# Residual input copied to the output by DMA and accumulated onto, with x reloaded as bf16 and the expert broadcast in another PSUM tile

## The reference

```python
x = x + hgrn(layernorm(x), Wi, Wf, Wg, g_norm_weight, Wo)
x = x + moe(layernorm(x), router_w, w1, w2, w3)

def hgrn(x):                      # all weights 2048 x 2048
    gate = sigmoid(x @ Wf.T); i_in = silu(x @ Wi.T) * (1 - gate)
    o = scan over tokens of o[t] = gate[t] * o[t-1] + i_in[t]
    g = x @ Wg.T
    return (g * rsqrt(mean(g*g) + EPS) * g_norm_weight * (o * sigmoid(o))) @ Wo.T

def moe(x):                       # 8 experts, top 2, d_ff 1024
    weights = softmax of the two largest router logits, 0 for the others
    return sum_e weights[e] * ((silu(x @ w1[e]) * (x @ w2[e])) @ w3[e])
```

## Time and profile before

| | us |
|---|---|
| median of 3 runs | 4249.4 |
| lowest of the runs | 4248.9 |
| the profiled execution | 4253.0 |
| its span on the slowest core (core 5) | 4251.1 |
| spans of the 8 cores | 4232.7 to 4251.1 |
| PE busy | 3777.4 (89%) |
| DVE busy | 1351.3 (32%) |
| ACT busy | 366.5 (9%) |
| POOL busy | 316.2 (7%) |
| mean granted TensorE clock | 0.95 |

### The profile page before, as it was taken

One profiled execution on the slowest core, in us unless ns is written; L12 is line 12 of the kernel. 1 busy time (PEld: TensorE's weight loads), 2 busy tenths in 40 slices (PEclk: granted clock), 3 DMA queues, 4 the chain that ended last, 5 costly groups with the idle time before them and its releaser, 6 DMA issues.

```text
span 4251.1 us, 43621 instructions; the slowest of 8 cores (4232.7 to 4251.1 us)
## 1 busy us (share of the span) xinstructions
PE 3777.4 (89%) x18832; PEld 1776.6 (42%) x18832; DVE 1351.3 (32%) x1154; ACT 366.5 (9%) x347; POOL 316.2 (7%) x358
## 2 busy tenths in 40 slices
PE   0998999989913899999999999999999999999992
PEld 0554444434412344444444444444444444444442
DVE  4322455532245223222222322322322222232233
ACT  3222121110020000000000000000000000000000
POOL 0000000000000001100100100100000010010011
PEclk9998999999956999999999999999999999999995
DMA  5122212112173233433433443344344344334239
GB/s 168 31 35 46 39 30 40 20 35 36 38 228 70 27 38 35 43 35 33 43 36 32 43 40 33 35 43 40 30 40 40 30 40 40 33 38 40 23 35 158
DMA packets 416189, 204.23 MB, mean 48 GB/s; under 512 B 399600, under 2 KB 399600, under 8 KB 407808
## 3 DMA queue, kind: packets, MB, share of 16 engines
q0 software_dynamic: 411216, 167.84, 32.4%
q1 hardware_dynamic: 4784, 33.61, 2.6%
HBM read 302.11 MB, written 33.55 MB: 79 GB/s over the span
## 4 chain that ended last, share of the span: by engine, by line
PE 81%; DVE 9%; DMA 6%; ACT 2%; issue 1%; DVEq 0%; POOL 0%; ACTq 0%; SPq 0%; POOLq 0%
PE pga L862 21%; PE pw L923 21%; PE pva L877 20%; PE po L566 5%; PE pg L327 5%; DMA y<-fsc 3%; PE pi L468 3%; PE pf L468 3%; DMA fsc<-x 2%; DVE fsc L500 2%; DVE fsc L507 1%; DVE bufB L508 1%; DVE bufA L252 1%; ACT fsc L504 1%; DVE fsc L608 0%
## 5 line engine op out<-in xcount | busy, mean ns | idle before, releaser
L862 PE MATMUL pga<-bufA,wsc 128*128 128x512 bf16 x4032 | 908.1, 384 | 12.4 <-DVE fsc L819 12.4
L923 PE MATMUL pw<-gvw,wsc 128*128 128x512 bf16 x4096 | 899.1, 383 | 20.5 <-DVE gvw L896 18.7
L877 PE MATMUL pva<-bufA,wsc 128*128 128x512 bf16 x4032 | 890.8, 379 | 0.0
L923 PEld LDWEIGHTS pw<-gvw,wsc 128*128 128x128 bf16 x4096 | 403.3, 99 | 516.3 <-issue 43.3
L862 PEld LDWEIGHTS pga<-bufA,wsc 128*128 128x128 bf16 x4032 | 398.0, 99 | 503.2 <-issue 39.4
L877 PEld LDWEIGHTS pva<-bufA,wsc 128*128 128x128 bf16 x4032 | 394.5, 98 | 475.7
L742 POOL DMA_DIRECT2D wsc<-w x256 | 258.1, 1009 | 2528.6 <-PE pga L862 1118.5
L935 DVE TENSOR_TENSOR bufB<-pw,bufB 128x1024 bf16<-128x1024 f32 x224 | 274.3, 1225 | 524.4 <-PE pw L923 524.4
L889 DVE TENSOR_TENSOR gvw<-fsc,pga 128x1024 bf16<-128x1024 f32 x126 | 153.9, 1221 | 796.1 <-ACT fsc L885 796.1
L885 ACT ACTIVATE fsc<-pga 128x1024 f32<-128x1024 f32 x126 | 129.1, 1024 | 2474.2 <-PE pga L862 2474.2
L893 DVE TENSOR_TENSOR scr<-pva,fsc 128x1024 bf16<-128x1024 f32 x126 | 154.3, 1225 | 568.2 <-PE pva L877 568.2
(11 more groups left out here) (123 smaller groups left out, 1407.3 us busy)
## 6 DMA issues: line engine op xcount, KB each, us to landing
wsc<-w POOLq DMA_DIRECT2D x128, 512.0 KB, 6.3
fsc<-x SPq DMA_DIRECT2D x32, 1024.0 KB, 6.5
y<-fsc POOLq DMA_DIRECT2D x32, 1024.0 KB, 8.6
wsc<-w POOLq DMA_DIRECT2D x128, 256.0 KB, 4.4
wsc<-wg POOLq DMA_DIRECT2D x16, 512.0 KB, 5.0
wsc<-wo POOLq DMA_DIRECT2D x16, 512.0 KB, 5.0
gvw<-wi POOLq DMA_DIRECT2D x16, 512.0 KB, 5.1
gvw<-wf POOLq DMA_DIRECT2D x16, 512.0 KB, 6.7
```

The lines of the kernel that those rows point to most:

```text
L862: ins = e.matmul(out=pga[:, n2 * 512:(n2 + 1) * 512], lhsT=lhsT, rhs=bufA[:, k * 2048 + nn:k * 2048 + nn + 512], start=(k == 0), stop=(k = ...
L877: ins = e.matmul(out=pva[:, n2 * 512:(n2 + 1) * 512], lhsT=lhsT, rhs=bufA[:, k * 2048 + nn:k * 2048 + nn + 512], start=(k == 0), stop=(k = ...
L923: ins = e.matmul(out=pws[_sl][:, n2 * 512:(n2 + 1) * 512], lhsT=lhsT, rhs=gvw[:, k * 2048 + nn:k * 2048 + nn + 512], start=(k == 0), stop= ...
```

## The change

The diff touches five places.

- Before anything else on SP's queue (behind three small constants) stands one DMA that copies all of x to y, HBM to HBM, with a semaphore of its own, `ypre`.
- In the residual stage the 16 loads on SP are gone. POOL issues, once `TE_B3` is reached, two DMAs that load x as bf16 into `bufB`: `xq0` the first 4 tiles, `xq1` the other 12. VectorE now scales PSUM into the `fsc` slot without adding x. The store to y has become an accumulating DMA. A second VectorE instruction adds the `fsc` slot to x in `bufB`, in place of the copy, and waits for `xq0` or `xq1`. The row sum has moved to a ScalarE pass of its own.
- The gate and value block of expert 0 that stood ahead of the loop is gone; the loop does it.
- The broadcast of the weight row goes through `pw0` in place of `pga`.
- At the end the slots are two bf16 tiles in `gvw` in place of the f32 tiles of `fsc`, and the accumulating DMA reads bf16.

```diff
@@ before the first x load @@
+        ypre.n += 16
+        on("sync", lambda e, _h=ypre.h: e.dma_start(out=yout, in_=xin).then_inc(_h, 16))
@@ residual stage @@
+            wait("gpsimd", te, TE_B3)
+            on("gpsimd", lambda e, _h=xq0.h: e.dma_start(
+                out=bufB[:, 0:4 * 2048].rearrange("p (t d) -> p t d", t=4),
+                in_=xin[0:4 * 128, :].rearrange("(t p) d -> p t d", p=128)).then_inc(_h, 16))
+            on("gpsimd", lambda e, _h=xq1.h: e.dma_start(
+                out=bufB[:, 4 * 2048:16 * 2048].rearrange("p (t d) -> p t d", t=12),
+                in_=xin[4 * 128:16 * 128, :].rearrange("(t p) d -> p t d", p=128)).then_inc(_h, 16))
             for t in range(TL):
-                slot = xs.load(lambda e, _t=t, _i=xs.k % 2: e.dma_start(
-                    out=xs_ap[_i], in_=xin[_t * 128:(_t + 1) * 128, :]))
...
-                v_r = emit("vector", lambda e, _i=i, _t=t, _sl=sl: e.scalar_tensor_tensor(
-                    out=xs_ap[_i], in0=slTs[_sl][:], scalar=st1(RMS, _t), in1=xs_ap[_i],
-                    op0=ALU.mult, op1=ALU.add), inc=ve)
+                v_r = emit("vector", lambda e, _i=i, _t=t, _sl=sl: e.tensor_scalar_mul(
+                    xs_ap[_i], slTs[_sl][:], st1(RMS, _t)), inc=ve)
                 slT_rel[sl] = v_r
                 wait("gpsimd", ve, v_r)
+                wait("gpsimd", ypre, 16)
                 spl = spill.load(lambda e, _i=i, _t=t: e.dma_start(
-                    out=yout[_t * 128:(_t + 1) * 128, :], in_=xs_ap[_i]))
-                v_cp = emit("vector", lambda e, _i=i, _t=t: e.tensor_scalar(
-                    bufB[:, _t * 2048:(_t + 1) * 2048], xs_ap[_i], 1.0, 0.0,
-                    ALU.mult, ALU.add, accum_out=st1(SUM, _t)), inc=ve)
+                    out=yout[_t * 128:(_t + 1) * 128, :], in_=xs_ap[_i],
+                    accum_op=ALU.add))
+                wait("vector", xq0 if t < 4 else xq1, 16)
+                v_cp = emit("vector", lambda e, _i=i, _t=t: e.tensor_tensor(
+                    out=bufB[:, _t * 2048:(_t + 1) * 2048], in0=xs_ap[_i],
+                    in1=bufB[:, _t * 2048:(_t + 1) * 2048], op=ALU.add), inc=ve)
                 wait("scalar", ve, v_cp)
                 emit("scalar", lambda e, _t=t: e.activation(
                     out=gvw[:, 0:2048], in_=bufB[:, _t * 2048:(_t + 1) * 2048],
+                    func=AF.Copy, accum_out=st1(SUM, _t)), inc=ac)
+                emit("scalar", lambda e, _t=t: e.activation(
+                    out=gvw[:, 0:2048], in_=bufB[:, _t * 2048:(_t + 1) * 2048],
                     func=AF.Square, accum_out=st1(SQ, _t)), inc=ac)
@@ experts @@
-                if e_ == 0:
-                    s1_0 = c1q[(0, 0)]
-                    s2_0 = c2q[(0, 0)]
...
                 for hb in range(2):
-                    if pga_rel is not None:
-                        wait("tensor", ve, pga_rel)
+                    if pw_rel[0] is not None:
+                        wait("tensor", ve, pw_rel[0])
...
-                            ins = e.matmul(out=pga[:, n2 * 512:(n2 + 1) * 512],
+                            ins = e.matmul(out=pw0[:, n2 * 512:(n2 + 1) * 512],
...
-                    pga_rel = emit("vector", lambda e, _hb=hb: e.tensor_copy(
-                        out=wb_ap[:, _hb * 1024:_hb * 1024 + 1024], in_=pga[:]), inc=ve)
+                    pw_rel[0] = emit("vector", lambda e, _hb=hb: e.tensor_copy(
+                        out=wb_ap[:, _hb * 1024:_hb * 1024 + 1024], in_=pw0[:]), inc=ve)
@@ end @@
+            ebuf = [gvw[:, 0:2048], gvw[:, 2048:4096]]
...
                 v_o = emit("vector", lambda e, _i=i, _sl=sl: e.tensor_copy(
-                    out=xs_ap[_i], in_=slEs[_sl][:]), inc=ve)
+                    out=ebuf[_i], in_=slEs[_sl][:]), inc=ve)
...
                 so = accs.load(lambda e, _i=i, _t=t: e.dma_start(
-                    out=yout[_t * 128:(_t + 1) * 128, :], in_=xs_ap[_i],
+                    out=yout[_t * 128:(_t + 1) * 128, :], in_=ebuf[_i],
                     accum_op=ALU.add))
```

More of the change, by code:

```diff
@@ L162, in build @@
         xs = Stream("xs", 2, "sync")
+        ypre = S("ypre")
+        xq0 = S("xq0")
+        xq1 = S("xq1")
         spill = Stream("sp", 2, "gpsimd")
@@ L587, in build @@
             slT_rel = [None, None]
+            wait("gpsimd", te, TE_B3)
+            xq0.n += 16
+            on("gpsimd", lambda e, _h=xq0.h: e.dma_start(
+                out=bufB[:, 0:4 * 2048].rearrange("p (t d) -> p t d", t=4),
+                in_=xin[0:4 * 128, :].rearrange("(t p) d -> p t d", p=128)).then_inc(_h, 16))
+            xq1.n += 16
+            on("gpsimd", lambda e, _h=xq1.h: e.dma_start(
+                out=bufB[:, 4 * 2048:16 * 2048].rearrange("p (t d) -> p t d", t=12),
+                in_=xin[4 * 128:16 * 128, :].rearrange("(t p) d -> p t d", p=128)).then_inc(_h, 16))
             for t in range(TL):
-                slot = xs.load(lambda e, _t=t, _i=xs.k % 2: e.dma_start(
-                    out=xs_ap[_i], in_=xin[_t * 128:(_t + 1) * 128, :]))
                 sl = t % 2
@@ L603, in build @@
                 vte = emit("tensor", tgrp, inc=te)
-                use("vector", slot)
+                i = t % 2
+                if xs.rel[i]:
+                    for (rs, rv) in xs.rel[i]:
+                        wait("vector", rs, rv)
+                    xs.rel[i] = None
                 wait("vector", te, vte)
                 wait("vector", ve, v_rms)
-                i = slot[0]
-                v_r = emit("vector", lambda e, _i=i, _t=t, _sl=sl: e.scalar_tensor_tensor(
-                    out=xs_ap[_i], in0=slTs[_sl][:], scalar=st1(RMS, _t), in1=xs_ap[_i],
-                    op0=ALU.mult, op1=ALU.add), inc=ve)
+                v_r = emit("vector", lambda e, _i=i, _t=t, _sl=sl: e.tensor_scalar_mul(
+                    xs_ap[_i], slTs[_sl][:], st1(RMS, _t)), inc=ve)
                 slT_rel[sl] = v_r
                 wait("gpsimd", ve, v_r)
+                wait("gpsimd", ypre, 16)
                 spl = spill.load(lambda e, _i=i, _t=t: e.dma_start(
-                    out=yout[_t * 128:(_t + 1) * 128, :], in_=xs_ap[_i]))
-                v_cp = emit("vector", lambda e, _i=i, _t=t: e.tensor_scalar(
-                    bufB[:, _t * 2048:(_t + 1) * 2048], xs_ap[_i], 1.0, 0.0,
-                    ALU.mult, ALU.add, accum_out=st1(SUM, _t)), inc=ve)
+                    out=yout[_t * 128:(_t + 1) * 128, :], in_=xs_ap[_i],
[4 more added lines that the diff above has]
+                    in1=bufB[:, _t * 2048:(_t + 1) * 2048], op=ALU.add), inc=ve)
                 wait("scalar", ve, v_cp)
@@ L760, in build @@
             c3q = {}
[L762 to L775, removed]
-            for e_ in range(NEXP):
-                if e_ == 0:
-                    s1_0 = c1q[(0, 0)]
-                    s2_0 = c2q[(0, 0)]
[L781 to L790, removed]
-                    wait("tensor", ve, pga_rel)
[L792 to L801, removed]
+            for e_ in range(NEXP):
                 wait("tensor", miscs, MISC_S)
@@ L818, in build @@
                     wait("vector", te, v_b)
-                    pga_rel = emit("vector", lambda e, _hb=hb: e.tensor_copy(
-                        out=wb_ap[:, _hb * 1024:_hb * 1024 + 1024], in_=pga[:]), inc=ve)
-                v_wb = pga_rel
-                if e_ == 0:
-                    wait("vector", te, v_v00)
-                    wait("vector", ve, v_wb)
-                    pva_rel = emit("vector", lambda e: e.tensor_tensor(
-                        out=vs_scr, in0=pva[:], in1=wb_ap[:, 0:1024], op=ALU.mult), inc=ve)
-                    emit("vector", lambda e: e.tensor_tensor(
-                        out=gvw[:, 0:1024], in0=gvw[:, 0:1024], in1=vs_scr, op=ALU.mult))
-                    wait("vector", te, v_v01)
-                    pw_rel[0] = emit("vector", lambda e: e.tensor_tensor(
-                        out=vs_scr, in0=pw0[:], in1=wb_ap[:, 1024:2048], op=ALU.mult), inc=ve)
-                    last_gv = emit("vector", lambda e: e.tensor_tensor(
-                        out=gvw[:, 1024:2048], in0=gvw[:, 1024:2048], in1=vs_scr,
-                        op=ALU.mult), inc=ve)
+                    pw_rel[0] = emit("vector", lambda e, _hb=hb: e.tensor_copy(
+                        out=wb_ap[:, _hb * 1024:_hb * 1024 + 1024], in_=pw0[:]), inc=ve)
+                v_wb = pw_rel[0]
                 for fm in range(TFm):
@@ L844, in build @@
                         c2q[(e_ + 1, 0)] = col_load(wc2, w2_d, e_ + 1, 0, c2sl[nb % 2], 16)
-                    if e_ == 0 and fm == 0:
-                        continue
                     s1 = c1q[(e_, fm)]
```

12 lines of the change are left out of this document (6 added, 6 removed).

## The result

| | before | after |
|---|---|---|
| lowest of the runs, us | 4248.0 | 4343.9 |
| ratio of after to before, 95% interval | | 1.022 [1.020, 1.024] |

The account below looks back on a forecast made before the run. The prediction took TensorE to bound the kernel, with DMA-heavy start, residual stage and end where PE nearly idles. Start +84, residual +6, experts -15, end -8 sum to +67 on the median 4249.4: forecast 4317 us, range 4272 to 4350.

Parts of the forecast that it names:

- The copy: Start: copying x to y ahead of the x loads takes 95 us (53 to 115), making the start 84 us later.
- rival (a): Start: the copy is slower, from 112 us upward, making the change slower by over 2%; chance 0.24.
- The estimate of 94 us: Start: copy time from 33.6 MB of reads plus writes at about 358 GB/s of HBM bandwidth per core.
- The shift of the x tiles: Start: tile 2 taken at 110 us instead of 25.70, later tiles at the old pace; +84 us.
- The order of the queue: Start: the 16 x loads stand wholly behind the copy on SP's queue, since engines consume a ring's descriptors in order.
- rival (c): Start: x loads and copy interleave, so the start is +50 instead of +84 and the time 4283; chance 0.11.
- The residual stage: Last po evacuation to last Square: accumulates wait behind xq1, then 6.41 us a tile; +6 us (-2 to +22).
- the 348 GB/s of source data: Residual stage: rate of casting x loads at share 1, from g stage loads; 16.78 MB take 48 us.
- The experts: Expert loop: weight row broadcast through pw0 removes a wait and part of a slow-clock cost; -15 us (-12 to -21).
- The second wait: Start of each expert: 1.55 us until pga is free for the first gate group; its removal saves 12.4 over eight.
- The end: Final stage: bf16 cast and accumulates reading 0.5 MB instead of 1 MB from SBUF; -8 us (-23 to -2).
- a model in which reading 4 KB less is 25% less: Final stage: accumulates priced by bytes read, 16 KB becoming 12, so 6.41 us a tile becomes 4.8; 23 us less.

Follow-up runs that it names:

- the probe: Two kernels with DMA phases put ahead of the kernel before, each waiting for the last; for 16.8 MB, merged copy 104.2 us, load 56.7, store 48.4, f32 accumulate 106.1.
- the best version of this change: The changed kernel with the copy of x to y cut in 16 pieces of 1 MB, one for each g block: ratio to before 0.9977.

## Why the prediction was wrong

I forecast 4317, 1.6% slower, and "within 2%" as the likeliest (0.61). It is 2.2% slower, 4342 by the ratio: inside the range, but most likely on the other side of the bound, on which the interval's lower end lies. The direction, and the mechanism of every part but the end, held; terms were mis-sized.

**The copy (the step that failed).** I took 95 us and it took 112.1, which is the mark that rival (a) named. Two errors. First, I treated the accumulate as almost a ceiling, because it has a stream more, and went below its 101. The probe shows that copy and accumulate cost the same, 104 and 106 with the queue kept full: both are a load plus a store, and the SBUF side isn't what counts. Second, I wrote that POOL's first weight loads "now land during the copy" and gave them no price: two blocks of 1.05 MB take 2 x 3.5 = 7 us of full engines, an estimate from the probe's load, and 104 + 7 = 111. They did lie beside the copy to its end: one of them took 113.8 us to land (core 5 of after, line of the weight loads):

```profile
DMA to landing us min/median/max: 4.9/5.1/113.8
```

The estimate of 94 us from the Trainium skill's HBM bandwidth (HBM Reference, Specifications) was too low as well: the copy alone took 104, and the measurement decides. The shift of the x tiles came nearly as worked: tile 2 is 9 us less late than the copy is long, where I had 11, and the tiles after it keep their pace on seven cores. Core 5 of before, from which I read the pace, was slower than they were.

**The order of the queue.** I argued that the x loads stand behind the copy on SP's ring, and that interleaving, rival (c), would save 34 us. On another ring, with small packets, they do interleave, and the kernel isn't faster. The ring was never the cost; (c) counted the tiles' delay and forgot that the copy's bytes still have to pass before the last tile.

**The residual stage, +10.6 for +6.** The pace (6.35 for 6.41), the accumulate behind xq1 (6.2 us after its landing, for 6.4) and the tail held. x took longer: the 348 GB/s of source data came from a window with the engines 0.23 busy; with all cores loading at once a load of 57 us gets 296. xq1 landed at 1255.3 + 55.5 = 1310.8, some 6 us later against the stage's start than I had it. That is about the lower bound of 300 GB/s that I had given.

**The experts, -20.2 for -15.** The second wait, 12.4, as read. From the broadcast to the first value group PE needs 12.07 us (2188.36 to 2200.43) instead of 14.61 (2082.26 to 2096.87): 2.5 us less, of which 1.55 is the wait and 0.9 the group behind it (8.77 for 9.70). I had allowed 0.4 for that. The windows of after (core 5) say where the 0.9 comes from:

```profile
2192.00:2194.00 2.00, 2.00 (x7) 0.80 (x6) 1.23 (x1) 0.00 (x0) 0.00 (x0) 0.61 0.84 88
2194.00:2196.00 2.00, 2.00 (x6) 0.71 (x5) 0.00 (x0) 0.00 (x0) 0.00 (x0) 0.53 0.01 1
2196.00:2198.00 2.00, 2.00 (x11) 0.88 (x9) 0.00 (x0) 0.00 (x0) 0.00 (x0) 1.00 0.00 0
```

In before the granted clock was 0.50 for all of 2086 to 2092 and 0.82 in the 2 us behind: the group, from 2087.34 on, ran some 5.4 us at the lower level. In after, where PE stood idle once and not twice, the granted clock averages 0.61 and 0.53 in two windows and is full again behind them, which makes some 3.4 us at the lower level. Half of the difference of 2.0 us is about the 0.9.

**The end, -2.1 for -8.** This is the one mechanism that I had wrong. My bound of -2 was right; I put weight on a model in which reading 4 KB less is 25% less, and the probe rules it out (107.2 us from bf16, 106.1 from f32).

With the copy at 112 the sum would have been +84, which is 2.0%; with xq1 6 us later as well, +90, against the +90.8 measured on core 5. That they meet so closely is partly luck. The errors of the experts (-5) and the end (+6) cancel, and so do core 5's outlier at the start (-4 against the corrected 101) and the +5 of two stages that the change doesn't touch. The copy alone takes the forecast to the bound.

**Slips in the working.** The chain of the residual stage repeats seven times on core 5, not eight. With x at 400 GB/s the stage comes out at 0, not -2. A third of 0.50 is 0.17, not 0.12: over 2% slower should have had 0.41 and within 2% 0.56. None changes the forecast.

## What to carry to other kernels

Count an accumulating DMA and an HBM to HBM copy as a load plus a store, as they cost here; the accumulate didn't get cheaper with a bf16 tile on the SBUF side. Before moving traffic, ask whether the stage is short of DMA time or of slots: a share of 0.7 with a wait in each cycle meant slots here, and more of them, with the tiles loaded ahead that they allow, were worth some 72 us by the median of the cores (13 at the start, 59 in the residual stage), where the best version of this change gained 10, all of it from the expert part. The bulk copy was free only beside compute and in pieces of 1 MB; in one piece it cost some 5 us with small packets and 34 us of the projections with large ones, because the loads that the compute waited for didn't get their turn.

## What the runs showed of the hardware

- 16.8 MB on eight cores at once: HBM to HBM 104 us in 64 KB packets, 117 in 8 KB packets; accumulate 106 to 107 from f32 or bf16; load 57, store 48, SBUF to SBUF 48.
- A load of 1 MB in 8 KB packets beside a copy in 64 KB packets on another ring landed after about 88 us (tile 0 taken at 91.6); beside a copy in 8 KB packets tiles came every 11 to 12 us.
- A weight load of 0.5 MB beside the copy in 64 KB packets took 48.9 us to land instead of 5.1.
- With enough DMAs in flight, loads and stores mixed reach 329 GB/s at share 0.99, near the 314 worked out from the share of 0.72 in before.
